# Node projection in the graph-table stage, edge terms stored in seven parts, first gathers from the counting stage on

## What is computed

```
hx = x_norm @ Wg                                   # node projection, heads of 64
al = leaky_relu((hx.as)[src] + (hx.ad)[dst] + (edge term))
te = relu(edge_attr @ We + be) * exp(x_norm @ Wo + bo)[src]   # edge term = te @ Wge . ae
al = softmax of al over the edges of each dst
out = segment_sum(hx[src] * al, dst)
```

## Time and profile before

| what | us |
|---|---|
| median of 3 runs (lowest, highest) | 2993.35 (2993.1, 2994.16) |
| span of the profiled execution | 2989.7 |
| median less span: what lies around it | 3.65 |
| graph tables (first instruction of counting) | 0 to 155.5 |
| counting (to the first of lookup) | 155.5 to 327.8 |
| lookup, edge weights, aggregate of layer 0 | 327.8 to 1034 |

### The profile page before, as it was taken

How to read it: one execution, slowest core, us unless ns; L and a number is a source line. 1 busy time by engine, 2 the same in 40 slices (tenths; PEclk the granted TensorE clock), 3 DMA queues, 4 the chain that set the end, 5 groups by cost and what they waited for, 6 DMA issues and landing times. The chain is left out here.

```text
span 2989.7 us, 39776 instructions
## 1 busy us (share of the span) xinstructions
PE 2211.4 (74%) x11685; PEld 1650.5 (55%) x11685; DVE 1789.0 (60%) x4141; ACT 948.0 (32%) x1705; POOL 1059.9 (35%) x1034
## 2 busy tenths in 40 slices
PE   5469563517888653368887389928999999997977
PEld 1136452205666451145655367726888888886646
DVE  6488897756777495457775344447444444434753
ACT  5435100211222101100000022227766666664422
POOL 0000576756777476757777333030000000000000
PEclk9789786758999766689998599968999999998987
DMA  4144673334555364345565399733565555561001
GB/s 182 14 136 164 214 234 104 116 110 136 164 158 157 123 226 123 118 124 156 161 168 140 119 340 386 238 91 98 147 158 147 136 148 147 143 153 46 1 15 46
DMA packets 368926, 432.55 MB, mean 145 GB/s; under 512 B 48543, under 2 KB 322944, under 8 KB 365542
## 3 DMA queue, kind: packets, MB, share of 16 engines
q1 hardware_dynamic: 269610, 224.54, 25.4%
q0 software_dynamic: 50496, 151.74, 17.5%
q10 hardware_dynamic: 48656, 54.31, 5.5%
HBM read 333.58 MB, written 97.72 MB: 144 GB/s over the span
## 5 line engine op out<-in xcount | busy, mean ns | idle before, releaser
L2386 PE MATMUL hop_sums<-hop_pieces,hop_weights 128*128 128x512 f32 x3125 | 714.9, 391 | 65.4 <-DVE hop_pieces L2274 65.2
L2386 PEld LDWEIGHTS hop_sums<-hop_pieces,hop_weights 128*128 128x128 f32 x3125 | 589.8, 189 | 190.4 <-DVE hop_pieces L2274 66.9
L2323 ACT ACTIVATE hop_weights<-col_columns 128x640 fp32r<-128x640 f16 x625 | 458.7, 738 | 225.2 <-PE hop_sums L2386 202.9
L521 POOL DMA_INDIRECT gat_ring<-hx_rows,src_i x392 | 436.6, 1114 | 163.3 <-issue 118.4
L521 POOL DMA_INDIRECT gat_ring<-hx_next,src_i x392 | 388.3, 991 | 150.5 <-issue 115.0
L1813 PE MATMUL agg_acc<-gat_ring,agg_oh 128*128 x976 | 265.6, 416 | 66.9 <-DVE agg_oh L1714 64.2
L1813 PE MATMUL agg_acc<-agg_msg,agg_oh 128*128 x976 | 246.3, 402 | 51.5 <-DVE agg_oh L1717 51.4
L1813 PEld LDWEIGHTS agg_acc<-gat_ring,agg_oh 128*128 128x128 f32 x976 | 179.7, 200 | 147.5 <-issue 127.4
L2443 POOL IOTA slc_valid<- 128x25 f32 x1 | 0.2, 162 | 735.1 <-POOLq L76 735.1
L1714 DVE TENSOR_SCALAR agg_oh<-agg_nodes,dst_f,w_cols 128x128 f32<-128x128 f32 x488 | 174.9, 406 | 122.0 <-PE agg_acc L1813 67.8
L1813 PEld LDWEIGHTS agg_acc<-agg_msg,agg_oh 128*128 128x128 f32 x976 | 179.7, 195 | 111.5 <-issue 86.4
(11 more groups left out here) (466 smaller groups left out, 3036.1 us busy)
## 6 DMA issues: line engine op xcount, KB each, us to landing
col_columns<-count_rows SPq DMA_DIRECT2D x60, 1600.0 KB, 8.0
look_part<-src_low SPq DMA_DIRECT2D x28, 896.0 KB
exp_w<-in_L_ffn_w SPq DMA_DIRECT2D x16, 1024.0 KB, 10.2
count_windows<-cnt_out SPq DMA_DIRECT2D x67, 200.0 KB, 1.9
count_windows<-cnt_out ACTq DMA_DIRECT2D x64, 200.0 KB, 1.9
staged<-gat_ring ACTq DMA_DIRECT2D x14, 520.0 KB
gat_ring<-staged SPq DMA_DIRECT2D x14, 520.0 KB, 3.8
agg_res<-x_norm ACTq DMA_DIRECT2D x50, 128.0 KB, 3.5
```

The costliest lines, as they stand in the source:

```text
L521: pool.indirect_dma_start(out=self.ring[:, 4 * slot + 2 * (q % 2) + k, :], out_offset=None, in_=self.g.hx_rows, in_offset=bass.IndirectOff ...
L2323: act.activation(weights[:, q % SLOTS_W, :, :], columns[n % STAGES][:, c * GROUP:(c + 1) * GROUP, b % 2 * P:(b % 2 + 1) * P], ACT.Copy).th ...
L2386: mm = pe.matmul(sums[m % BANKS][:, :], weights[:, q % SLOTS_W, i, :], pieces[k % 2][:, t, :], start=(t == 0), stop=(t == NB - 1))
```

## The change

Four things move. The node projection (`FirstRows`) leaves the counting stage and is woven into the 49 steps of the graph-table loop, one block in every step instead of every second window: statistics in steps 4 to 8, normalizing from step 12, turning from 13, projecting from 14, copying out from 15 on. The edge terms are stored in seven parts, each after its four rounds; the banks for the outcome of a round go from two to one, and the zero fills and the store of the split sources are spread over the steps. Gathers of layer 0 begin in counting: 48 pairs (24 quads) there, all of them put away by SP between the stores of the windows; 56 pairs in lookup, which fill the whole ring; none in edge weights; the remaining 92 pairs in aggregate (112 before).

```diff
@@ graph_tables
-        edges = edge_terms(s, g, io, [s.ps(f"edge_ps{n}") for n in range(6)])
+        edges = edge_terms(s, g, io, [s.ps(f"edge_ps{n}") for n in range(5)])
+        rows = FirstRows(s, g, io["x"])
...
                 sp.dma_start(dst_i[:, :], io["dst_cols"]).then_inc(loaded, 16)
-                sp.dma_start(g.src_i[:, :], io["src_cols"]).then_inc(loaded, 16)
+                edges["load"](sp, lambda: rows.load(sp, io))
                 sp.dma_start(src_rows[:, :], io["src_rows"]).then_inc(src_came, 16)
                 sp.dma_start(src_turned[:, :], io["src_turned"].rearrange("(p j) -> p j", p=P)).then_inc(src_came, 16)
-                edges["load"](sp)
+                sp.dma_start(g.src_i[:, :], io["src_cols"]).then_inc(src_here, 16)
+                for j in steps:
+                    rows.on_sync(sp, j)
+                    if 10 <= j < 10 + len(fills):
+                        fill_with_zeros(sp, j - 10)
+                    if j == SPLIT_AT + 1:
+                        sp.wait_ge(src_split, after(1))
+                        sp.dma_start(g.src_low.rearrange("(p j) -> p j", p=P), src_low[:, :]).then_inc(src_kept, 16)
+                        sp.wait_ge(src_split, after(2))
+                        sp.dma_start(g.src_high.rearrange("(p j) -> p j", p=P), src_high[:, :]).then_inc(src_kept, 16)
+                    for c in range(edges["parts"]):
+                        if j == min(edges["step_of"](c), steps[-1]):
+                            edges["store"](sp, c)
+                edges["all_stored"](sp)
+                rows.all_kept(sp)
+                sp.wait_ge(src_here, after(16))
...
-                with dve.Fori(0, ET // GRP // 2) as m:
-                    group(2 * m, 0)
-                    group(2 * m + 1, 1)
-                group(ET // GRP - 1, 0)
+                for n in steps:
+                    group(n, n % 2)
+                    rows.on_vector(dve, rows_link, n)
+                    if n == SPLIT_AT:
+                        split_sources()
...
+                rows.tables_on_vector(dve, rows_link)
...
-                edges["scalar"](act)
+                edge_round, copy_out = edges["scalar"](act)
+                done = 0
+                for j in steps:
+                    rows.row_on_scalar(act, j)
+                    if (j + 1) * edges["rounds"] // len(steps) > done:
+                        edge_round(done)
+                        done += 1
+                    rows.turn_on_scalar(act, j)
+                copy_out(edges["rounds"] - 1)
                 act.wait_ge(table, after(1))
                 nc.scalar.activation(t1[:, :], t1[:, :], ACT.Sqrt).then_inc(rooted, 1)
+                rows.tables_on_scalar(act)
...
                     if (n + 1) * edges["rounds"] // (ET // GRP) > done:
                         edge_round(done)
                         done += 1
+                    rows.on_tensor(pe, n)
@@ edge_terms
         for c in range(LOADS):
+            if c == 1:
+                others()
...
+    def step_of(c):
+        return -(-(c + 1) * (ROUNDS // LOADS) * (ET // 8) // ROUNDS) + 1
+
+    def store(sp, c):
+        sp.wait_ge(copied, after((c + 1) * (ROUNDS // LOADS)))
         for k in range(GROUPS):
-            sp.dma_start(g.edge_terms[:, k * PER:(k + 1) * PER], terms[k * ED:k * ED + HT, :]).then_inc(stored, 16)
-        sp.wait_ge(stored, after(16 * GROUPS))
+            at_ = k * PER + c * PART
+            sp.dma_start(g.edge_terms[:, at_:at_ + PART], terms[k * ED:k * ED + HT, c * PART:(c + 1) * PART]).then_inc(stored, 16)
+
+    def all_stored(sp):
+        sp.wait_ge(stored, after(16 * GROUPS * LOADS))
...
-            if r >= 2:
-                pe.wait_ge(copied, after(r - 1))
+            pe.wait_ge(copied, after(r))
             for k in range(GROUPS):
-                mm = pe.matmul(down[r % 2][k * ED:(k + 1) * ED, 0:WIDE], v[:, :], hid[k][r % 2], start=True, stop=True,
+                mm = pe.matmul(down[k * ED:(k + 1) * ED, 0:WIDE], v[:, :], hid[k][r % 2], start=True, stop=True,
@@ Gather
-    AHEAD = ((56, 69, 71, 84), (34, 42, 46, 56))
-    EVERY = (5, 0)
-    BACK, LEAD = 4, 10
+    AHEAD = ((48, 104, 104, 104, 104), (0, 34, 42, 46, 56))
+    STAGED = (24, 0)
+    BACK, LEAD, PUTS = 4, 10, 4
...
+        count = self.early = self.STAGED[layer]
+        self.staged = [HELD + (i + 1) * (QUADS - HELD) // count - 1 for i in range(count)]
+        self.per_put = -(-count // self.PUTS)
...
+    def put_at(self, i):
+
+        return (i + 1) * Counter.MAIN // self.early
+
+    def put_away(self, eng, i):
+        for half in range(2):
+            self.wait_came(eng, 2 * i + half)
+        eng.dma_start(self.g.staged[i], self.ring[:, 4 * i:4 * i + 4, :]).then_inc(self.put[i // self.per_put], 16)
+
+    def wait_put(self, eng, i):
+
+        k = i // self.per_put
+        eng.wait_ge(self.put[k], after(16 * len(range(k * self.per_put, min((k + 1) * self.per_put, self.early)))))
@@ FirstRows
-    FEED, TURN, PRODUCT, ROW_AT, EVERY = 8, 9, 11, 12, 2
-    XS = 3
+    STATS, FEED, TURN, PRODUCT, ROW_AT, EVERY = 4, 12, 13, 14, 15, 1
+    XS = 4
...
-    def on_scalar(self, act, j):
-        if j == 5:
+    def row_on_scalar(self, act, j):
+        if j == self.STATS + len(self.came) + 1:
...
+    def turn_on_scalar(self, act, j):
@@ counts
-                rows.load(sp, io)
+                put = 0
                 for j in windows:
                     c.store(sp, j)
-                    rows.on_sync(sp, j)
+                    while put < g.gather.early and j >= g.gather.put_at(put):
+                        g.gather.put_away(sp, put)
+                        put += 1
+                while put < g.gather.early:
+                    g.gather.put_away(sp, put)
+                    put += 1
                 c.all_stored(sp, c.MAIN)
-                rows.all_kept(sp)
...
+                g.gather.on_gpsimd(pool, g.gather.upto[0])
...
-                for j in windows:
-                    c.on_vector(dve, range(j, j + 1))
-                    rows.on_vector(dve, rows_link, j)
-                rows.tables_on_vector(dve, rows_link)
+                c.on_vector(dve, windows)
@@ lookup, edge_weights
-                g.gather.on_gpsimd(pool, g.gather.upto[0])
-
-            if g.gather.staged:
-                @block.scalar
-                def _(act):
-                    g.gather.put_away(act)
+                g.gather.on_gpsimd(pool, g.gather.upto[1])
...
-                g.gather.on_gpsimd(pool, g.gather.upto[1])
+                g.gather.on_gpsimd(pool, g.gather.upto[2])
```

More of the change, by code:

```diff
@@ L157, in graph_tables, with fill_with_zeros @@
         src_came, src_split, src_kept = s.sem("src_came"), s.sem("src_split"), s.sem("src_kept")
[L159 to L170, removed]
+        words = NE * SLOTS * (D + 1) // P
+        fills = [(g.edge_fill, 0, 2048), (g.edge_fill, 2048, ET * SW)] + [
+            (g.expert_in, lo, min(lo + 2048, words)) for lo in range(0, words, 2048)]
+        def fill_with_zeros(sp, n):
+            if not n:
+                sp.wait_ge(filled, after(1))
+            what, lo, hi = fills[n]
+            sp.dma_start(what.rearrange("(p j) c -> p (j c)", p=P)[:, lo:hi], zero[:, 0:hi - lo]).then_inc(filled, 16)
         with s.block() as block:
@@ L436, in copy_out, with edge_round @@
             act.wait_ge(downed, after(r + 1))
-            act.activation(terms[:, cols(r)], down[r % 2][:, 0:WIDE], ACT.Copy).then_inc(copied, 1)
-        for r in range(ROUNDS):
+            act.activation(terms[:, cols(r)], down[:, 0:WIDE], ACT.Copy).then_inc(copied, 1)
+        def edge_round(r):
             act.wait_ge(upped, after(r + 1))
@@ L491, in __init__ @@
         self.upto = self.AHEAD[layer]
-        every = self.EVERY[layer]
-        self.staged = list(range(HELD + every - 1, QUADS, every)) if every else []
-        self.held = [HELD - len(self.staged) + i for i in range(len(self.staged))]
+        count = self.early = self.STAGED[layer]
+        self.staged = [HELD + (i + 1) * (QUADS - HELD) // count - 1 for i in range(count)]
+        self.per_put = -(-count // self.PUTS)
         quads = self.staged + [k for k in range(QUADS) if k not in self.staged]
@@ L500, in __init__ @@
         self.in_order, self.freed = s.sem("in_order"), s.sem("freed")
-        self.put, self.back = s.sem("put"), [s.sem(f"back{k}") for k in range(self.BACK)]
+        self.put, self.back = ([s.sem(f"{n}{k}") for k in range(m)] for n, m in (("put", self.PUTS), ("back", self.BACK)))
         s.arm()
@@ L511, in on_gpsimd @@
             quad, away = q // 2, n < 2 * len(self.staged)
-            slot = self.held[n // 2] if away else quad % HELD
+            slot = n // 2 if away else quad % HELD
             if n >= FLIGHT:
                 self.wait_came(pool, n - FLIGHT)
-            if not away and quad < HELD and quad in self.held and not q % 2:
-                pool.wait_ge(self.put, after(16 * len(self.staged)))
```

(29 more changed lines are left out.)

62 lines of the change are left out of this document (26 added, 36 removed).

## The result

The changed kernel takes 3047.97 us (median of 4 runs, 3045.98 to 3050.99), the kernel before 2993.22 beside it (2989.77 to 2994.16): ratio 1.0182, 95% interval 1.017 to 1.0193, against a forecast of 3046. The profiled execution spans 3044.2 us, 54.5 more than before.

A forecast was written before the change was run, and what follows sets the result against it. No engine is full in the graph tables; a loop of waits between ACT and PE sets the pace. Terms 71 + 11 - 1.4 + 25 - 23 - 17 - 13 = +53 on 2993.35 give 3046 us; 8-in-10 range 2998 to 3085.

The forecast's parts named there:

- part 5: Counting: windows and gathers go in step, 6.0 us a quad, 155 us instead of 172.3: -17, bounds -37 and -9.
- Blocks in series: Graph-table steps 13 to 39: node blocks add to the loop of waits, 6.47 us a round step: +71 us.
- Statistics and weights: Graph-table steps 4 to 12: DVE's statistics and weight operations cost +11 us; the loop starting earlier gives -1.4.
- The clock: Graph-table round steps: PE idles, its clock falls, and half of its 3.4 us doubles: +25 us, bounds 0 and 68.
- The tail: End of graph tables: edge terms stored in parts shorten the 36.1 us behind the loop: -23 us, bounds -10 and -24.
- an end of some 9: Counting: about 9 us at its end for the last landing and POOL's one write, 5.5 us.
- Rival D: Counting: each gather stops DVE for 0.94 us by the lock; stage 225 us, +53 instead of -17; total 3116 us; chance 0.02.
- 6 and 7: Lookup: nothing; edge weights: nothing, up to -5 us; aggregate: 40 fewer gathers, the waits for a quad go, -13 us.
- A (overlap): Graph-table steps 13 to 39: blocks overlap rounds, +17 instead of +71, no clock gap; total 2967 us; chance 0.10.
- B: Gathers keep up in counting (-37) and PE's clock holds in graph tables (no cost): total 3001 us; chance 0.12.
- C: PE's clock stays low through graph-table steps 13 to 39, +68 for +25: total 3089 us; chance 0.04.

The follow-up runs named there:

- the idle matmuls: Changed kernel plus 36 unneeded matmuls on PE in each round step from step 13, while PE waits for the relus: 3029.92 us, ratio 1.0119.
- The other order: Changed kernel with PE doing the node block before the round and ACT after it, in each graph-table step: 2990.14 us, ratio 0.9994.
- The later puts: Changed kernel with each put in counting four windows later in SP's order, still 96 gathers: 3039.28 us, ratio 1.0152.
- the fastest kernel: Kernel before with edge terms stored in parts, 17 quads put away in lookup, six more pairs gathered in edge weights: 2962.16 us, ratio 0.9896.

## Why the prediction was right, and where it was off

The mechanisms came as forecast, with one term mis-sized (part 5). That the sum lies within 2 us is in part luck: by the stages the graph tables came out 3.1 us under the forecast, counting 6.0 over, lookup and edge weights 1.4 under, the aggregate 0.4 over.

**1. Blocks in series: right.** With the clock held by the idle matmuls a round step is 6.16 us (forecast 6.47), one without a round 2.28 (2.38), and steps 13 to 39 take 117.3 us for 50.5 before: +66.8 for +70.5. The turned copy and the row copies take ACT 0.6 us in all up to the relus (147.35 to 147.95), where I had counted 0.39 and 0.5. The other order, with the same work and the clock at 1.00, leaves +33 of this; the other half is the series.

**2. Statistics and weights: a little more.** The relus of step 13 start at 61.68 instead of 48.26, +13.4, where 11 - 1.4 was forecast. DVE's five steps with statistics take 3.05 us each (3.15 forecast); the first relus start 0.56 later than before, so the earlier start of 1.4 us did not come, which is half of the miss.

**3. The clock: right.** Steps 13 to 39 take 90.7 us more than before (141.2 for 50.5); 66.8 is the series, so 23.9 the clock, for +25. It is the edge layer that runs at half clock; the block behind it is already at full clock.

**4. The tail: right in kind, beyond its bound.** 234.96 - 224.85 = 10.1 us for 36.1, -26.0, against -23 and a bound of -24. DVE's tables start less than 1 us behind the last copy (224.85), and the small node tables lie within what I had added.

**5. Counting: the step that was mis-sized.** Gathers and windows go in step, as forecast, and a quad takes (374.26 - 236.47) / 24 = 5.74 us for 6.0. But "an end of some 9" left out two things: DVE's search for open items, which follows the last window, and the 7 us more that the stage takes to end behind POOL's indirect DMAs. From the last gather to the end it is 22 us. Rival D of the same prediction counts 20 us behind the last window, with the search in it; this term did not. So -6 on the gathers and +13 at the end: -11 for -17, within the bounds. The later puts, which lay the search beside the gathers, gave 7 us of it back.

**6 and 7. Lookup, edge weights, aggregate: right.** Lookup and edge weights are -1.4 in sum, the aggregate -12.6 for -13. DVE's waits for a quad fell by 10.9; where the other 1.7 come from is not shown. That the gain goes with the waits and not with the place of the gathers is borne out twice: without gathers in counting, waits and aggregate are both back (13.1 and 359.2 us), and the fastest kernel has waits of 2.9 and nearly the same short aggregate with no gather in counting.

**The rivals.** A (overlap) needs another order; with it steps 13 to 39 cost 33 us more than before (relus of round 7 at 61.60, of round 22 at 145.18, 83.6 us for 50.5), not 17: I had bounded them by ACT alone. What bounds them there is not shown (from step 13 to the last copy PE is busy for 81 of 103 us, ACT for 70). B fails on both counts: the gathers don't keep up and the clock falls. C fails by the clock of 1.00 in the projection's stretch. D, the lock: windows beside gathers in the changed kernel stay at their pace, and gathers are stretched:

```profile
297.12 0.68 DVE L744 TENSOR_TENSOR cnt_dst_hot<-cnt_count,cnt_key 128x512 f16<-128x512 f16 x1
297.31 1.31 POOL L555 DMA_INDIRECT gat_ring<-hx_rows,src_i  x1 [0.30 <-issue]
...
298.74 0.68 DVE L744 TENSOR_TENSOR cnt_dst_hot<-cnt_count,cnt_key 128x512 f16<-128x512 f16 x1
```

A window takes 1.62 us beside gathers, against 1.61 without, and a gather 1.31 for 0.95. Of the rule in the Trainium skill ("SBUF — State Buffer", section "SBUF: two separate sides") the half that DVE holds up GpSimd agrees; that a gather holds up DVE is not seen here.

## What to carry to other kernels

Work that is small on every engine can still cost its whole length when two engines' orders put it in series with a loop of waits: write down one step of each engine's order, add the links, and try the order in which each engine does the other job while it waits. A gap that this opens on PE can cost again, at half clock, what PE does next (1.6 us a step here). Transfers brought forward paid here only up to the waits that they took away (13 us), and stores that queued behind their landing cost 7 us of their stage (by the later puts). A stage that hung on the last of many indirect DMAs on POOL ended late here; one in which POOL was done sooner did not.

## What the runs showed of the hardware that was not expected

- 36 idle matmuls in a gap of 2.7 us made the next 3.5 us of matmuls 1.6 us shorter: 23.9 us in steps 13 to 39, 20.9 in the stage.
- A stage with 64 or 96 indirect DMAs on POOL ended 10.2 to 13.1 us behind POOL's last write, one without them 4.7 to 5.5, and 96 memsets don't change that. In a stage whose last indirect DMA on POOL came 16 us before its end, no such time showed. The cause is open.
